# A nine-stage language tower on one core: the 16-expert gate moved into the expert stage, code-book weights loaded one stage earlier, attention's last batch finished by VectorE

## The reference

```python
h = h + L0_ffn(layernorm(h), router_w, w1, w2)        # 16 experts: 8 of width 128, 8 of width 256
#   probs = softmax(x @ router_w.T); the 8 largest kept and scaled to sum 1
#   out = sum_e gate[:, e] * (gelu(x @ w1[:, e]) @ w2[e])
...
h = h + L2_ffn(layernorm(h), P, C, W1, b1, W2, b2, G1, g1b, G2, g2b)
#   x projected (P) into 8 subspaces of 16; 64 codes C each; the 4 best codes weigh 64 small
#   networks 16 -> 32 -> 16 (W1, W2); then a small closing network (G1, G2)
...
h = h + L3_attn(layernorm(h), w_qkv, scale, w_out, b_out)
#   12 heads; per row only the larger logits are kept, softmax over them
```

## Time and profile before

| | |
|---|---|
| median of 3 runs | 3295.45 us (3294.97 to 3295.58) |
| the profiled execution, its own time | 3295.63 us |
| its span from first to last instruction | 3293.8 us |
| mean granted TensorE clock | 0.858 of full |
| busy share of the span: PE, DVE, ACT, POOL | 72%, 69%, 48%, 32% |

### The profile page before, as it was taken

How to read it: one execution, slowest core, us unless ns; L and a number is a source line. 1 busy time by engine, 2 the same in 40 slices (tenths; PEclk the granted TensorE clock), 3 DMA queues, 4 the chain that set the end, 5 groups by cost and what they waited for, 6 DMA issues and landing times. The chain is left out here.

```text
span 3293.8 us, 39013 instructions
## 1 busy us (share of the span) xinstructions
PE 2360.9 (72%) x12580; PEld 1429.7 (43%) x12620; DVE 2278.2 (69%) x5846; ACT 1592.2 (48%) x2954; POOL 1046.5 (32%) x578
## 2 busy tenths in 40 slices
PE   5859994888888876799821112788889788773456
PEld 4646662334334334599611112322222466663345
DVE  5753334898989996211379996688888699997521
ACT  3221113667675652111217773677778556655111
POOL 2000002888898983577100000000000033443032
PEclk9969996899999998899955555899999899997578
DMA  2230002222222223311100000344435400000321
GB/s 55 37 118 1 1 0 98 78 103 103 78 103 92 96 96 87 117 41 40 58 0 0 0 1 15 116 129 142 147 122 186 131 1 1 1 1 1 129 79 57
DMA packets 86535, 219.13 MB, mean 67 GB/s; under 512 B 35709, under 2 KB 53339, under 8 KB 76891
## 3 DMA queue, kind: packets, MB, share of 16 engines
q1 hardware_dynamic: 80188, 204.38, 18.4%
q0 software_dynamic: 6144, 12.25, 1.2%
HBM read 199.46 MB, written 25.03 MB: 68 GB/s over the span
## 5 line engine op out<-in xcount | busy, mean ns | idle before, releaser
L2467 DVE TENSOR_TENSOR_SCAN mam_st<-mam_da,mam_st 128x512 f32<-128x512 f32 x384 | 441.1, 1204 | 39.4 <-ACT mam_da L2407 35.7
L2235 POOL TENSOR_TENSOR mam_st<-mam_du,mam_b_rows 128x1536 f32<-128x1536 f32 x128 | 442.4, 3457 | 79.7 <-PE mam_ysum L2305 55.7
L2305 PE MATMUL mam_ysum<-mam_st,held_ident 128*128 128x512 f32 x768 | 366.0, 615 | 0.0
L1863 ACT ACTIVATE cod_hp<-cod_up,cod_b 128x512 f32<-128x512 f32 x512 | 316.7, 703 | 83.5 <-PE cod_up L1724 83.3
L2407 ACT ACTIVATE mam_da<-mam_delta,mamw_decay 128x508 f32<-128x508 f32 x384 | 251.6, 681 | 177.6 <-DVE mam_st L2467 142.2
L2606 POOL TENSOR_TENSOR att_probs<-att_se,att_neg 128x1536 f32<-128x1536 f32 x16 | 55.0, 3440 | 811.2 <-DVE att_neg L2816 811.2
L2305 PEld LDWEIGHTS mam_ysum<-mam_st,held_ident 128*128 128x128 f32 x768 | 151.2, 199 | 153.7 <-issue 150.3
L692 DVE SCALAR_TENSOR_TENSOR held_h<-x_dn,held_gate,held_h 128x192 f32<-128x192 f32 x256 | 89.1, 411 | 182.6 <-PE x_dn L659 180.9
L2816 DVE MATCH_REPLACE8 att_neg<-att_top,att_neg 128x128 f32<-128x128 f32 x768 | 201.1, 276 | 0.3 <-issue 0.3
L2005 DVE TENSOR_TENSOR cod_hp<-cod_hp,cod_gate 128x512 f32<-128x512 f32 x256 | 164.0, 683 | 46.4 <-ACT cod_hp L1863 45.9
L1724 PE MATMUL cod_up<-cod_zr,cod_w1r 96*128 96x512 bf16 x512 | 180.2, 391 | 15.6 <-ACT cod_hp L1863 9.3
(11 more groups left out here) (552 smaller groups left out, 5366.0 us busy)
## 6 DMA issues: line engine op xcount, KB each, us to landing
cod_wide_gates<-gate_scratch SPq DMA_DIRECT2D x128, 512.0 KB, 3.9
mam_b_rows<-b_scratch SPq DMA_DIRECT2D x32, 1024.0 KB, 6.8
mam_c_rows<-b_scratch SPq DMA_DIRECT2D x32, 1024.0 KB, 4.7
slot_scratch<-in_slot_fresh SPq DMA_DIRECT2D x2, 3860.0 KB, 14.3
sw_w<-in_L_w SPq DMA_DIRECT2D x1, 6144.0 KB, 18.5
grw_w<-in_L_w SPq DMA_DIRECT2D x1, 5376.0 KB, 42.7
grw_w<-in_L_w SPq DMA_DIRECT2D x1, 4608.0 KB
sw_w<-in_L_w SPq DMA_DIRECT2D x1, 4608.0 KB, 31.4
```

What stands on the lines that cost most here:

```text
L1863: nc.scalar.activation(hp[step % HOLD][:, j, :], up[u % BANKS][:], ACT.Gelu_apprx_tanh, bias=b1[:, sub * HT + f:sub * HT + f + 1]).then_in ...
L2235: nc.gpsimd.tensor_tensor(st[it % N_ST][:], du[r % 2][:], along(b_rows[:, p % RING, n % PIECE, :], 1, [P, MC, MT]), ALU.mult)\
L2305: last = nc.tensor.matmul(ysum[:, c, :], m.ident[:], st[it % N_ST][:, c, :], start=False, stop=(it % DS == DS - 1))
L2467: nc.vector.tensor_tensor_scan(fs, fa, fs, 0.0, ALU.mult, ALU.add).then_inc(scanned, 1)
```

## The change

There are three edits in one. First, the gate of `n1` moves into `experts_stage`: VectorE does it there before its adds, TensorE runs 12 pairs of up products (`AHEAD`) ahead of the down products, not one, and the ring `ht` has 28 tiles. Second, `proj`, `codes`, `sel_w` and both halves of `w1` are loaded by SyncE in `n5`, into tiles of a new outer stage `codw`; VectorE splits the first half at the end of its list of `n5` (`tail`), the second at the start of `cod`; TensorE spreads the first half after the first split, and waits for the other loads only after that. Third, for the last batch of the attention GpSimd's two functions and ScalarE's `normalise` are left out, and VectorE does their work in four passes.

```diff
-    E, NT, NUP, NHT = len(tiles), sum(tiles), 4, 4
+    E, NT, NUP, NHT = len(tiles), sum(tiles), 4, 28
+    AHEAD, HB = NT // 2, NB // 2
...
-            up_products(0, 0)
+            for i in range(AHEAD):
+                up_products(*pairs[i])
             for i, (g, p) in enumerate(pairs):
-                if i + 1 < len(pairs):
-                    up_products(*pairs[i + 1])
+                if i + AHEAD < len(pairs):
+                    up_products(*pairs[i + AHEAD])
...
         def _(v):
+            c = Chain(v, dve)
+            c.step(nc.vector.memset(gate.work[:], 0.0))
+            for k in range(2):
+                gate.steps(nc, c, m, slice(k * HB, (k + 1) * HB))
             for g in range(NG):
...
+def split_w1(nc, v, w, h):
+    x, part = w.w1[:, h], [p[:, h] for p in w.w1_part]
+    base = 3 * h
+    v.wait_ge(w.w1_in[h], 16)
+    nc.vector.tensor_copy(part[0], x).then_inc(w.split_own, 1)
+    v.wait_ge(w.split_own, base + 1)
+    nc.vector.tensor_tensor(x, x, part[0], ALU.subtract).then_inc(w.split_own, 1)
...
-            pe.wait_ge(w_in, 16 * N_IN)
             pe.wait_ge(w1_split, 1)
             for i in range(N_W // 2):
                 spread_w1(i, first_turn(first_w(i)))
+            pe.wait_ge(w_in, 16 * N_IN)
             for sub in range(SS):
                 spread_z(0, sub, first_turn(FIRST_ZR + sub), first_ready)
+            pe.wait_ge(w1_split, 2)
...
-    norm_stage(nc, m, a, "n5")
-    codes_stage(nc, m, a)
+    with Stage(nc, "codw") as s:
...
+        norm_stage(nc, m, a, "n5", ahead=[
+            (w.w1[:, 0], a["S_w1"][:, 0], w.w1_in[0]), (w.proj[:], "S_proj", w.p_in), (w.codes[:], "S_codes", w.p_in),
+            (w.sel_w[:].bitcast(I16), "sel_w", w.p_in), (w.w1[:, 1], a["S_w1"][:, 1], w.w1_in[1])],
+            tail=lambda v: split_w1(nc, v, w, 0))
+        codes_stage(nc, m, a, w)
...
-            for b in range(NB):
+            for b in range(NB - 1):
                 logits(b)
                 bar(b)
...
+            def last_logits():
+                b = NB - 1
+                x, cut = probs[b % 2][:], neg[b % NRING][:]
+                v.wait_ge(searched, b + 1)
+                v.wait_ge(pt_ready, b - 1)
+                c.step(nc.vector.tensor_tensor(x, along(se[b % NRING][:], 1, heads), cut, ALU.subtract))
+                c.step(nc.vector.scalar_tensor_tensor(x, cut, BAR, x, ALU.add, ALU.min))
+                nc.vector.tensor_reduce(down[b % 2][:], x, AX.X, ALU.max, negate=True).then_inc(lifted, 1)
+
+            def last_normalise():
...
+                nc.vector.tensor_tensor(x, x, along(part[b % 2][:], 2, heads), ALU.mult).then_inc(probs_ready, 1)
...
-            highest(NB - 1)
+            last_logits()
             invert(NB - 1)
+            last_normalise()
```

More of the change, by code:

```diff
@@ L336, in _ @@
                     gate.steps(nc, c, m, half(k))
+            if tail is not None:
+                tail(v)
         @block.tensor
@@ L614, with experts_stage @@
     pass
-def experts_stage(nc, m, a, name, tiles, func, w1_sb, w2_sb, w_in, wide):
-    E, NT, NUP, NHT = len(tiles), sum(tiles), 4, 4
+def experts_stage(nc, m, a, name, tiles, func, w1_sb, w2_sb, w_in, wide, gate):
+    E, NT, NUP, NHT = len(tiles), sum(tiles), 4, 28
+    AHEAD, HB = NT // 2, NB // 2
     first = [sum(tiles[:e]) for e in range(E)]
@@ L629, in experts_stage @@
         dn_ready, dn_added = s.sem("dn_ready"), s.sem("dn_added")
+        dve = s.sem("dve")
+        gate.tiles(s, HB)
         block = s.block()
@@ L1606, in _ @@
         def _(sp):
[L1607 to L1610, removed]
+            for dst, src in ((sel_z[:].bitcast(I16), "sel_z"),
                              (sel_g[:].bitcast(I16), "sel_g"), (b2, "S_b2"), (b2d[:], "S_b2d"), (b1[:], "S_b1"), (w2[:], "S_w2"),
@@ L2081, in s_l2ffn @@
 def s_l2ffn(nc, m, a):
-    norm_stage(nc, m, a, "n5")
-    codes_stage(nc, m, a)
+    with Stage(nc, "codw") as s:
+        w = Loads()
+        w.proj, w.codes = s.sb("proj", [DC, 2, 2 * P]), s.sb("codes", [P, 2, 4 * SM])
+        w.sel_w = s.sb("sel_w", [P, 4, NPART, KR], BF16)
+        w.wide_gates = s.sb("wide_gates", [P, GRING, QD, GT])
+        w.hp = [s.sb(f"hp{i}", [P, QS, GT]) for i in range(HOLD)]
+        w.w1 = w.wide_gates[:].rearrange("p i j t -> p (i j t)")[:, 0:2 * SM * SH].rearrange("p (h f) -> p h f", h=2)
+        w.w1_part = [x[:].rearrange("p j t -> p (j t)").bitcast(BF16).rearrange("p (h f) -> p h f", h=2) for x in w.hp]
+        w.p_in, w.split_own, w.w1_split = s.sem("p_in"), s.sem("split_own"), s.sem("w1_split")
+        w.w1_in = [s.sem(f"w1_in{h}") for h in range(2)]
+        norm_stage(nc, m, a, "n5", ahead=[
[3 more added lines that the diff above has]
+        codes_stage(nc, m, a, w)
 DI, DS, DT, TAPS = 2 * D, 16, 12, 4
@@ L2624, in _ @@
                     add_out(b - 2)
+            add_out(NB - 3)
             add_out(NB - 2)
@@ L3529, in s_l0ffn @@
         w_in = s.sem("w_in")
-        norm_stage(nc, m, a, "n1", router="L0_router", n_routes=16, gate=Gate(16, 8, True), wide=wide,
+        norm_stage(nc, m, a, "n1", router="L0_router", n_routes=16, wide=wide,
                    ahead=((w1_sb[:], "L0_w1", w_in), (w2_sb[:], "L0_w2", w_in)))
-        experts_stage(nc, m, a, "x1", tiles, ACT.Gelu_apprx_tanh, w1_sb, w2_sb, w_in, wide)
+        experts_stage(nc, m, a, "x1", tiles, ACT.Gelu_apprx_tanh, w1_sb, w2_sb, w_in, wide, Gate(16, 8, True))
 def s_l1ffn(nc, m, a):
```

40 lines of the change are left out of this document (19 added, 21 removed).

## The result

| | before | after | less |
|---|---|---|---|
| first measurement, medians (4 runs each) | 3295.21 us | 3264.49 us | 30.7 us, ratio 0.9904 [0.9889, 0.992] |
| second, beside the experiments (17 and 4 runs) | 3297.80 us | 3262.78 us | 35.0 us, ratio 0.989 [0.9876, 0.9905] |
| third (13 and 4 runs) | 3297.79 us | 3265.68 us | 32.1 us, ratio 0.9903 [0.9886, 0.9919] |
| the profiled execution of the first | 3295.63 us | 3264.58 us | span 3293.8 to 3262.8 us: 31.0 |

A forecast was written before the change was run, and what follows sets the result against it. No engine was above 72% busy; barriers separate stages, so time cut from a stage's chain is cut from the whole. 16.2 + 11.9 + 6.4 = 34.5 us less than 3295.63 gave 3261.1, against the median 3261; range 3255 to 3269.

The forecast's parts named there:

- Start of `x1`, 17.4 earlier: End of `n1`: with the gate gone, `x1` starts at 204.88 instead of 222.28, 17.4 us earlier.
- The rule by which TensorE enters `x1` at the full clock: Rival at `x1`'s start: sustained activity releases the throttle, first pair 2.97 us, 1.5 us more gain, 3259.5; chance 0.08.
- Gate hidden by 13 up pairs: In `x1`: the gate is ready 10.9 us before the first down products, behind 13 pairs of up products.
- The low clock for 13 pairs: Rival in `x1`: up products running alone stay at 1.2 GHz, 38.7 us more, no gain, 3298; chance 0.03.
- The adds, 1.2 us: End of `x1`: four narrow pairs lose 0.30 each, VectorE's adds 2.90 against TensorE's 2.60; 1.2 us lost.
- Code book, 11.9: `n5` and `cod`: moving the loads and half the split earlier gives 11.9 us less (4.9 to 12.3).
- The term's upper bound of 12.3: `n5` and `cod`: the most that the code book's edit was said to give, 12.3 us.
- the extra border: End of `cod`: the outer stage adds a second border, taken as 0.5 us (0.3 to 0.9).
- the rival of a low clock there: `cod`: TensorE stays at 1.2 GHz through the first 16 pieces, so the edit gives 4.9, 3268; chance 0.12.
- Last batch, 6.4: End of the attention: VectorE doing the last batch's passes gives 6.4 us less, 4.8 at least.
- The product with the reciprocal: Last batch: 1.75 on VectorE and 0.05 of wait replace 3.70 in ScalarE's list, 1.85 us less.
- Untouched stages keep their length: All stages without edits: no change of length; a changed one was named as a sign of being wrong.

The follow-up runs named there:

- `e_A`: The kernel before with only the edit that moves the gate into `experts_stage` (and its caller); 3281.55 us, ratio 0.9945.
- `e_B`: The kernel before with only the code book's loads and split changed; 3286.36 us, ratio 0.9963.
- `e_oldwarm`: The kernel before plus 22 products whose result nobody reads, on TensorE ahead of the second last batch's turns; 3297.72 us, ratio 1.0.
- `e_warm`: The changed kernel plus 22 products whose result nobody reads, on TensorE ahead of the second last batch's turns; 3261.35 us, ratio 0.9888.

## Why the prediction was right, and where its terms were off

The sign, the places and the mechanisms held: each of the three edits shortened the stage that the forecast named, and by the wait that it named. Against 34.5 us there stand 30.7, 35.0 and 32.1. How near the total came is in part chance, as the list shows.

- **Start of `x1`, 17.4 earlier:** right. 17.64 in `e_A`, with `n1` at the clock that the forecast assumed; 20.1 in the first profile by a higher clock in `n1`, of which the low start of the first pair took 1.05 back.
- **The rule by which TensorE enters `x1` at the full clock:** it didn't. The first pair took 5.53 us, in `e_A` 4.90; that rival falls.
- **Gate hidden by 13 up pairs:** right, 11.5 us of cover against 10.9. The low clock for 13 pairs, the rival on the other side, didn't come: the pairs from 207.76 on take 2.97.
- **The adds, 1.2 us:** mis-sized. 2.1 by the rows of the four pairs, and 3.31 - 1.05 = 2.26 by `x1`'s whole length. The step set 2.90 of adds against 2.60 of products and forgot the handover, 0.23 for each pair, that two PSUM buffers don't hide. That `x1` shrank by about 1 us with 9 pairs ahead fits.
- **Code book, 11.9:** right, 12.3 in the first profile, 12.1 in the next two and 13.5 in `e_B`, where the projection took 5.37 us instead of 6.76. (The term's upper bound of 12.3 was a slip: 12.4 less its own smallest border of 0.3 is 12.1.) `mid_z` came 12.9 earlier (12.4 forecast), the extra border took 0.4 (0.5), the spread pieces had the full clock, and the rival of a low clock there falls.
- **Last batch, 6.4:** mis-sized, 5.25 up to the turns. The step took ScalarE's `keep_mixed` from a row of before in which the narrow products ran at 1.53 us. In all seven profiles of the new code without the unread products there they ran at 2.83. Once GpSimd's passes are gone this 1.3 us is on the path; `e_B` and `e_oldwarm` show that it wasn't before. The product with the reciprocal was right: recip to turns 2.07 us instead of 3.93, 1.86 against 1.85.
- **Untouched stages keep their length:** this is where the sum was too sure; the forecast named a changed length there as a sign of being wrong, and it showed. The scan stage took 758.6 to 760.4 us in four profiles of programs whose part up to there is that of before, and 756.6 to 761.7 in nine with the new `x1`; the attention's end takes 11.4 to 14.7 from the turns on, in old and new code; `n3` to `n5` takes 743.5 to 747.4, and `n1` starts between 169.3 and 172.8. In the attention and in `n1` the rows show the granted clock as the cause, in the scan stage for 2.9 of 4.5 us. In the first profile these differences cost 2.2 in the scan stage and its norm and 2 at the attention's end, and gave 2.4 in `n1`.

With `n1` at the clock that the forecast assumed, and the narrow products at the one that they had in all seven profiles, the change is worth 17.6 - 2.3 + 12.3 + 5.25 = 32.9 us; what separates the three measurements from it, 2.2, 2.1 and 0.8, is less than these differences from run to run.

## What to carry to other kernels

A row of before gives a duration at the clock which that stretch happened to have. Ahead of a sum, ask for each TensorE row on the new path whether it was behind an idle time, and put in both levels; a gap that another engine hid becomes a term once that engine is taken out. Where the same buffers pass between two engines in small pieces, the period can be the slower one's work plus the handover, as the 3.12 us here against 2.89. And a term below 2 us is judged by the spans of its stage in two or three profiles, not by one difference of times.

## What the runs showed of the hardware

TensorE was busy for 11.94 or 11.95 of 12 us in `n1` in each of these profiles, and was granted 0.50 or 0.64 in the same code (and the windows from 182 and from 185 above). The Trainium skill's rule that activity ends the low clock (TensorE: Matmul & The Clock Gate, Part 1) doesn't fit these rows, though it fits those of `e_warm`; what makes the difference, no run here shows.

GpSimd's clearing of a bfloat16 tile and VectorE's cast from float32 did not get on side by side: the cast that started 0.04 us behind the clearing ended at 2045.65, 1.08 us behind the clearing's end at 2044.57, while alone it takes 1.23. The Trainium skill (SBUF — State Buffer, SBUF: two separate sides) says that GpSimd and VectorE, the latter in modes that use two ports, share a pair of ports which one of them holds for a whole instruction while the other stands still; the rows with and without the overlap agree. That the cast runs in such a mode, no row shows.
